# Two kinds of tiles of the first stage mixed three to two, the first two windows loaded between them, and edge loads issued ahead of window loads

## What is computed

```python
h = jnp.concatenate([n_embed[senders], n_embed[receivers]], axis=-1)
h = jnp.tanh(h @ W0 + b0)
h = jnp.tanh(h @ W1 + b1)
h = h @ W2 + b2
h = h * (e_embed @ Wg)
return _segment_mean(h, senders, n_embed.shape[0])
```

## Time and profile before

| | |
|---|---|
| median of 3 runs | 2468.64 us (2465.61 to 2472.03) |
| the profiled execution, own time | 2466.78 us |
| its span, first to last instruction | 2465.0 us |
| first stage, until the last `TB` store has landed | 0 to 97.2 us |
| second stage, first window product to last `first_hidden` | 102.1 to 1603 us |
| mean granted TensorE clock | 0.888 |

### The profile page before, as it was taken

How to read it: one execution, slowest core, us unless ns; L and a number is a source line. 1 busy time by engine, 2 the same in 40 slices (tenths; PEclk the granted TensorE clock), 3 DMA queues, 4 the chain that set the end, 5 groups by cost and what they waited for, 6 DMA issues and landing times.

```text
span 2465.0 us, 41568 instructions
## 1 busy us (share of the span) xinstructions
PE 1989.2 (81%) x12990; PEld 1757.5 (71%) x12990; DVE 1594.8 (65%) x4240; ACT 1416.0 (57%) x2926; POOL 1473.5 (60%) x1204
## 2 busy tenths in 40 slices
PE   7799999999999999999999999945155655555560
PEld 6699889999999999989999989943144444444450
DVE  6466666666666666666666666654266566666575
ACT  2488888888888888888888888834011111111112
POOL 0327777777776777767777777423555555555503
PEclk9899999999999999999999999977567767776785
DMA  6888877777777777777777777574344544444413
GB/s 209 282 208 184 193 165 164 167 163 170 159 158 155 161 158 158 159 157 160 158 160 158 160 159 156 112 186 126 91 113 121 128 112 118 119 119 115 120 48 108
DMA packets 236177, 370.91 MB, mean 150 GB/s; under 512 B 35853, under 2 KB 168935, under 8 KB 235949
## 3 DMA queue, kind: packets, MB, share of 16 engines
q0 software_dynamic: 101232, 188.20, 38.7%
q1 hardware_dynamic: 134717, 179.94, 24.7%
HBM read 270.57 MB, written 97.45 MB: 149 GB/s over the span
## 4 chain that ended last, share of the span: by engine, by line
PE 56%; issue 18%; DVE 11%; ACT 5%; DMA 5%; another core or an unknown queue 4%; POOL 1%; SPq 0%; DVEq 0%; ACTq 0%; POOLq 0%
PE bank L1412 12%; PE bank L1410 12%; PE bank L1411 12%; PE bank L1462 4%; PE bank L1453 4%; DMA accA<-ystage,to_a 3%; PE bank L1479 2%; DVE in_window L860 2%; PE bank L1503 2%; PE bank L1514 2%; PE bank L1504 2%; PE bank L1515 2%; PE bank L1578 1%; ACT drop L1849 1%
## 5 line engine op out<-in xcount | busy, mean ns | idle before, releaser
L1306 POOL DMA_INDIRECT accA<-ystage,to_a x391 | 649.7, 1662 | 233.8 <-issue 111.6
L1312 POOL DMA_INDIRECT GA<-TA,src_c x391 | 426.7, 1091 | 323.3 <-issue 95.4
L1341 POOL DMA_INDIRECT Hg<-HT,src_c x391 | 372.9, 954 | 335.6 <-DVE xb L912 174.8
L1849 ACT ACTIVATE drop<-neg_m 128x1 f32<-128x1 f32 x98 | 28.9, 295 | 613.1 <-issue 348.2
L1410 PE MATMUL bank<-h1h,W1h 128*128 128x512 f32 x882 | 349.2, 396 | 1.5 <-DVE h1l L536 1.4
L1412 PE MATMUL bank<-h1h,W1l 128*128 128x512 f32 x882 | 348.3, 395 | 0.0
L1411 PE MATMUL bank<-h1l,W1h 128*128 128x512 f32 x882 | 347.3, 394 | 0.0
L536 DVE TENSOR_TENSOR h2l<-h2f,h2h 128x512 fp32r<-128x512 f32 (+1 forms) x294 | 202.9, 690 | 202.6 <-issue 78.9
L1607 PE MATMUL bank<-diag,ones 128*128 128x128 f32 x196 | 66.5, 435 | 306.3 <-DVE diag L896 250.2
L1617 PE MATMUL bank<-xb,in_window 128*128 128x260 f32 (+1 forms) x782 | 292.9, 542 | 1.1 <-issue 1.1
L536 DVE TENSOR_TENSOR h1l<-h1f,h1h 128x512 fp32r<-128x512 f32 x294 | 195.1, 691 | 131.3 <-ACT h1h L1686 114.2
(11 more groups left out here) (208 smaller groups left out, 5196.0 us busy)
## 6 DMA issues: line engine op xcount, KB each, us to landing
TW<-TB SPq DMA_DIRECT2D x196, 203.0 KB
ef<-in_eT SPq DMA_DIRECT2D x97, 256.0 KB
bcast_i<-in_src_row SPq DMA_DIRECT2D x97, 256.0 KB
HB<-hist SPq DMA_DIRECT2D x98, 130.0 KB
rel<-RL SPq DMA_DIRECT2D x97, 128.0 KB
rem<-RD SPq DMA_DIRECT2D x48, 256.0 KB
TB<-stB SPq DMA_DIRECT2D x24, 406.0 KB
accA<-zeros SPq DMA_DIRECT2D x4, 1677.0 KB, 13.1
```

What stands on the lines that cost most here:

```text
L1306: return pool.indirect_dma_start(out=table, out_offset=bass.IndirectOffsetOnAxis(ap=rows, axis=0), in_=sums, in_offset=None, compute_op=AL ...
L1312: pool.indirect_dma_start(out=GA[0:n, b % (GAR * BLOCKS_PER_GROUP), :].bitcast(f32), out_offset=None, in_=TA, in_offset=bass.IndirectOffse ...
L1341: pool.indirect_dma_start(out=Hg[0:n, slot, :], out_offset=None, in_=HT, in_offset=bass.IndirectOffsetOnAxis(ap=src_c[0:n, b:b + 1], axis= ...
```

## The change

- `STEPS` is the order of the 50 products: of five steps, the numbers 0, 2 and 4 are senders' tiles and 1 and 3 receivers'. The 25th sender's tile is step 40, steps 41 to 49 are receivers' tiles. TensorE, VectorE and SP follow it; the bank goes by the step.
- ScalarE moves six receivers' tiles ahead of its copies of the weights `W1`, `W2` and `Wg`.
- SP loads window 0 after step 32 (when ten receivers' tiles have landed) and window 1 after step 40. Their first rows are clipped so that they lie in those ten tiles; if a window lay elsewhere, the flag `outside` would send the whole kernel to its slow path. With these edges it stays 0.
- `wait_stage_n0` is split: at the start of the second stage the engines wait for the products alone (`wait_products_n0`), and for the stores (`wait_stores_n0`) at step 1, SP after `ef` and `bcast_i` of group 0. Buffers are laid out anew so that what is written early doesn't lie on `stA` and `stB`.
- In SP's loop window `g + 2` stands behind `ef` and `bcast_i` of group `g`.
- VectorE: one more small operation for `low2_i`, two for `early`, one later for the flag; `h1s` is cleared within the first stage, the constants of `mh` and `ml` at step 1.

```diff
+        early = sb("early", [P, 3])
...
+        EARLY = 10
+        steps_s, steps_r, STEPS = [], [], []
+        while len(STEPS) < 2 * NT:
+            sender = len(steps_s) < NT and len(STEPS) % 5 in (0, 2, 4)
+            (steps_s if sender else steps_r).append(len(STEPS))
+            STEPS.append(("sender" if sender else "receiver", len(steps_s if sender else steps_r) - 1))
+
+        def early_stores(slot):
+            return 16 * sum(len(pieces(t)) for t in range(slot, EARLY, N0R))
...
-        def wait_stage_n0(eng):
+        def wait_products_n0(eng):
+
+            eng.wait_ge(s_n0, 2 * NT)
+            eng.wait_ge(s_n0a, NT)
+            eng.wait_ge(s_n0l, NT)
+            eng.wait_ge(s_rd, 16 * RDS)
+            eng.wait_ge(s_wl, 4)
+
+        def wait_stores_n0(eng):
 
             for k in range(N0R):
                 eng.wait_ge(s_ta[k], stores(N0R, k))
                 eng.wait_ge(s_tb[k], stores(N0R, k))
-            eng.wait_ge(s_rd, 16 * RDS)
-            eng.wait_ge(s_pad, 16)
-            eng.wait_ge(s_wl, 4)
...
-            for t in range(4):
-                sender_bias(t)
+
+            def staged(p):
+                kind, t = STEPS[p]
+                if kind == "sender":
+                    sender_bias(t)
+                else:
+                    receiver_lo(t)
+
+            for p in range(4):
+                staged(p)
...
-            const(dve.tensor_scalar(low2_i[:, :, :], low_all[:, 2:4, :], 2.0, None, ALU.mult), "low_i")
+
+            const(dve.tensor_scalar(low2_i[:, :, TWR:NG], low_all[:, 2:4, TWR:NG], 2.0, None, ALU.mult))
+            const(dve.tensor_scalar(low2_i[:, :, 0:TWR], low_all[:, 2:4, 0:TWR], 2.0, float(2 * EARLY * P - P),
+                                    ALU.mult, ALU.min), "low_i")
...
-            for t in range(4, NT):
-                sender_bias(t)
-                if t == 10:
+
+            const(dve.tensor_tensor(early[:, 0:TWR], low_all[:, 2, 0:TWR], low_all[:, 3, 0:TWR], ALU.max))
+            const(dve.tensor_reduce(early[:, 2:3], early[:, 0:TWR], AX.X, ALU.max))
+            for p in range(4, 2 * NT):
+                staged(p)
+                if p == 20:
...
+                if p == 36:
+                    dve.wait_ge(s_wl, 4)
+                    const(dve.memset(h1s[:, :, :].bitcast(f32), 0.0))
+                if p == 33:
...
-            wait_stage_n0(dve)
-            const(dve.memset(h2l[2 * Q:P, :, 2, :].bitcast(f32), 1.0))
-            const(dve.memset(mh[:, :, :, OUT:OUT + 1].bitcast(f32), 1.0))
-            const(dve.memset(mh[:, :, :, OUT + 1:AW].bitcast(f32), 0.0))
-            const(dve.memset(h1s[:, :, :].bitcast(f32), 0.0))
-            const(dve.memset(ml[:, :, :, OUT:AW].bitcast(f32), 0.0), "ones")
-
-            for s in range(-2, NG + 1):
+            window_hot(0)
+            wait_products_n0(dve)
+            const(dve.memset(h2l[2 * Q:P, :, 2, :].bitcast(f32), 1.0), "ones")
+
+            for s in range(-1, NG + 1):
+                if s == 1:
+                    wait_stores_n0(dve)
+                    const(dve.memset(mh[:, :, :, OUT:OUT + 1].bitcast(f32), 1.0))
+                    const(dve.memset(mh[:, :, :, OUT + 1:AW].bitcast(f32), 0.0))
+                    const(dve.memset(ml[:, :, :, OUT:AW].bitcast(f32), 0.0), "sums' constants")
...
+            const(dve.scalar_tensor_tensor(worst[:, 2:3], early[:, 2:3], float(P - 1 - EARLY * P + HW), worst[:, 2:3],
+                                           ALU.add, ALU.max))
...
-            for t in range(NT):
-                n = rows_of_tile(t)
-                sp.wait_ge(s_n0a, t + 1)
-                for r, e in pieces(t):
-                    sp.dma_start(TA[t * P + r:t * P + e, :], stA[r:e, t % N0R, :]).then_inc(s_ta[t % N0R], 16)
-            for t in range(NT):
-                n = rows_of_tile(t)
-                sp.wait_ge(s_n0l, t + 1)
-                for r, e in pieces(t):
-                    sp.dma_start(TB[t * P + r:t * P + e, :].rearrange("p (k d) -> p k d", k=2),
-                                 stB[r:e, t % N0R, :, :].bitcast(f32)).then_inc(s_tb[t % N0R], 16)
...
-            wait_stage_n0(sp)
-            load_window(0)
-            load_window(1)
+            for p, (kind, t) in enumerate(STEPS):
+                n = rows_of_tile(t)
+                if kind == "sender":
+                    sp.wait_ge(s_n0a, t + 1)
+                    for r, e in pieces(t):
+                        sp.dma_start(TA[t * P + r:t * P + e, :], stA[r:e, t % N0R, :]).then_inc(s_ta[t % N0R], 16)
+                else:
+                    sp.wait_ge(s_n0l, t + 1)
+                    for r, e in pieces(t):
+                        sp.dma_start(TB[t * P + r:t * P + e, :].rearrange("p (k d) -> p k d", k=2),
+                                     stB[r:e, t % N0R, :, :].bitcast(f32)).then_inc(s_tb[t % N0R], 16)
+                if p == 32:
+
+                    for k in range(N0R):
+                        sp.wait_ge(s_tb[k], early_stores(k))
+                    sp.wait_ge(s_xl, PARTS)
+                    sp.wait_ge(s_rd, 16 * RDS)
+                    load_window(0)
+                if p == 40:
+                    load_window(1)
+            wait_products_n0(sp)
             for g in range(NG):
...
-                if g + 2 < NG:
-                    load_window(g + 2)
...
                 sp.dma_start(bcast_i[:, g % 2, 0:n],
                              src_row[g * GE:g * GE + n].partition_broadcast(P)).then_inc(s_bc[g % 2], 16)
+                if g == 0:
+                    for k in range(N0R):
+                        sp.wait_ge(s_tb[k], stores(N0R, k))
+                    sp.wait_ge(s_pad, 16)
+                if g + 2 < NG:
+                    load_window(g + 2)
...
-                t, half = u % NT, u // NT
+                kind, t = STEPS[u]
+                half = 0 if kind == "sender" else 1
                 n = rows_of_tile(t)
                 pe.wait_ge(s_xl, part_of_tile[t] + 1)
                 if u >= 8:
-                    if u - 8 < NT:
-                        pe.wait_ge(s_n0a, u - 8 + 1)
+                    kind, before = STEPS[u - 8]
+                    if kind == "sender":
+                        pe.wait_ge(s_n0a, before + 1)
                     else:
-                        pe.wait_ge(s_n0l, u - 8 - NT + 1)
+                        pe.wait_ge(s_n0l, before + 1)
...
+            def receiver_hi(t):
+                n = rows_of_tile(t)
+                act.wait_ge(s_n0, steps_r[t] + 1)
+                if t >= N0R:
+                    act.wait_ge(s_tb[t % N0R], 16 * (t // N0R))
+                copy(stB[0:n, t % N0R, 0, :], bank_n0(steps_r[t])[0:n, 0:H0]).then_inc(s_n0b, 1)
+
+            for t in range(6):
+                receiver_hi(t)
...
-            for t in range(NT):
-                n = rows_of_tile(t)
-                act.wait_ge(s_n0, NT + t + 1)
-                if t >= N0R:
-                    act.wait_ge(s_tb[t % N0R], 16 * (t // N0R))
-                copy(stB[0:n, t % N0R, 0, :], bank_n0(NT + t)[0:n, 0:H0]).then_inc(s_n0b, 1)
+            for t in range(6, NT):
+                receiver_hi(t)
...
-            wait_stage_n0(act)
-            act.wait_ge(s_dc, DC["ones"])
+            wait_products_n0(act)
...
+                if s == 0:
+                    act.wait_ge(s_dc, DC["ones"])
+                if s == 1:
+                    wait_stores_n0(act)
+                    act.wait_ge(s_dc, DC["sums' constants"])
```

25 lines of the change are left out of this document (11 added, 14 removed).

## The result

The changed kernel takes 2462.5 us (median of 15 runs, 2454.1 to 2470.2), the kernel before beside it 2470.7 us. The ratio is **0.9964, 95% interval 0.9952 to 0.9976**: 0.36% or 9 us less. The forecast was 2443 us, with 2436 to 2454 as its range: 25.6 us less than the kernel before, of which about a third came. One run in all of what follows, of e11, took 2717.8 us against 2441 to 2454 of its other five and is left out of its ratio.

A forecast was written before the change was run, and what follows sets the result against it. TensorE's pace was taken to bound the second stage, whose start waited for the first stage's stores and window load. From 2466.78 us, -19.6 (start) and -6 (edge loads) gave 2441.2, plus 1.9 for the median: 2443 us, range 2436 to 2454.

The forecast's parts named there:

- TensorE's products: First stage: mixed order lets TensorE run without stopping at 1.11 us a product, all done at 76.1 us.
- The gathers come later: First stage's end: last sender's tile moved at 66.8 us, POOL's gathers start at 70.4, the first group lands at 78.3.
- The last nine receivers' tiles: First stage's tail: 1.77 us a tile beside gathers, 25th tile moved at 81.9 us, first window product at about 82.5.
- the rule that the prediction took from the Trainium skill: DMA engines serve queues in turn, a packet each: 2.06 us a tile, start at 83.7 us; not used for the forecast.
- The start as a whole: Second stage's start: first window product at about 82.5 us instead of 102.13, worth -19.6 us.
- rival B: First stage: slower tail or TensorE stalling on full slots, start effectively 5 us later, ef about 1 us; 2453 us, chance 0.18.
- What followed the start: Second stage: runs at TensorE's pace, so an earlier start moves all behind it to the left; no loss was counted.
- Rival C: Second stage: earlier start, but what follows isn't at TensorE's pace; scatters keep the old end; 2462 to 2469 us, chance 0.06.
- two signs of being wrong: Second stage: a first window product behind 90 us, or a period still over 15.5 us, would show the forecast wrong.
- Edge loads a group earlier: Second stage's loop: SP reaches ef a whole group ahead of need, shortening the period; -6 us, bounds 0 and 7.2.
- Rival D: Second stage's loop: the new order makes each group wait on bcast_i; 2491 us at 0.5 us a group, chance 0.03.
- The sum: Whole kernel: 2466.78 - 19.6 - 6 = 2441.2 us profiled; runs' median 1.9 us above, so 2443 us.

The follow-up runs named there:

- e11: Changed kernel with groups 2 to 5 gathered no more than two groups ahead, run in the slower setting; ratio 0.9924 against the kernel before.
- e7: Changed kernel with windows 0 and 1 loaded behind the last TB store, in the faster setting; ratio 0.9932 against the kernel before.
- e10: Changed kernel with windows 0 and 1 behind the last TB store and groups 2 to 5 gathered at most two ahead, slower setting; ratio 0.9938.
- e3: Changed kernel with the gathers of groups 1 to 3 held until VectorE has moved the last receiver's tile, slower setting; ratio 0.9988.
- e9: Changed kernel unchanged, run again in the slower setting; ratio 0.9957 against the kernel before.
- e17: Changed kernel with window 0 after step 40, window 1 after the last store, groups 2 to 5 gathered at most two ahead, slower setting; 0.9927, 2445.8 us.
- e16: Changed kernel with window 0 loaded after step 40 and window 1 after the last TB store, slower setting; ratio 0.9947.
- e18: Changed kernel unchanged, run a third time in the slower setting; ratio 0.9964 against the kernel before.
- e12: Changed kernel with windows 0 and 1 loaded by GpSimd instead of SP, faster setting; ratio 0.9928 against the kernel before.
- e2: Changed kernel with SP's old loop order, window loads ahead of edge loads, from group 1 on, slower setting; ratio 0.9978.
- e14: e6 with window loads ahead of the edge loads again from group 1 on, faster setting; ratio 0.9964 against the kernel before.
- e1: Kernel before with one edit, window g + 2 behind ef and bcast_i of group g in SP's loop, slower setting; ratio 0.9988.
- e4: Changed kernel with the gathers of groups 2 and 3 held until first_hidden(0) is through, slower setting; ratio 0.9975.
- e6: Changed kernel with groups 2 to 5 gathered no more than two groups ahead, run in the faster setting; ratio 0.9935.

## Why the prediction was wrong

**TensorE's products.** Nearly right: done at 78.0 us against 76.1 forecast, with two short stops of 0.4 and 0.6 us. ScalarE's weight copies and the clear cost nothing.

**The gathers come later.** This term was mis-sized. The prediction moved the last sender's tile at 66.8 us; it was moved at 72.4 (70.4 and 70.5 in the other two profiles). It named window 1's hold on SP and forgot window 0's, which stands ahead of step 40 and held SP for 4.1 us, and it left the windows' bytes out of the DMA engines' account from 60 to 78 us. Without them (e7, e10) the move is at 68.1, so the windows are 4.3 of the 5.6 us (2.3 to 2.4 against the other two profiles); the other 1.3 are open. The landing of the group, taken as 3 us between 1 and 6, is 5.3 us here (83.33 to 88.59) and 4.6 to 6.8 us in the experiments: the upper bound was the nearer.

**The last nine receivers' tiles.** From the last sender's move to the last receiver's: 15.1 us forecast, 15.9 measured. The stores took 7 us each and not 3.1, by the chain of waits,

```profile
70.22 6.85 DMA TB<-stB
78.30 7.14 DMA TB<-stB
```

but four slots overlap them. From the tile moved at 77.69 us to the last, five tiles took 10.6 us, 2.1 each, beside gathers; I had 1.77. From 83 to 89 us the queues share nearly alike:

```profile
q1 hardware_dynamic: 403, 1.16, 52.0%
q0 software_dynamic: 318, 1.03, 49.7%
```

By the rule that the prediction took from the Trainium skill (page "DMA: Bandwidth & Descriptors", section "Queues, rings and completion order"), the engines serve the queues in turn, and a tile would take 2.06 us. The trace is near it here: 52.0% to 49.7%, and 2.1 us a tile. The kernel before is not, and not because its gathers had only begun: all sixteen were issued from 60.65 to 80.6 us, and the stores had 57.6% from 66 to 72 us and 60.2% from 72 to 78 us, the gathers 44.8% and 41.2%. What decides between the two shares is not shown, and neither is that the gathers set the tiles' pace: in e3, with four of them beside the tail in place of eight, the last five tiles took 12.5 us (74.03 to 86.54).

**The start as a whole.** First product at 89.4 in place of 82.5, 6.9 us late: 5.6 of it by step 40, 0.8 by the tail, the rest by the hand-overs. Alone this would be rival B ("the tail is slower", or "TensorE's products stall"), whose 5 us were near.

**What followed the start.** This step failed outright: the prediction let the 19.4 us from the first product to `eh(1)` stand, and no term stood for it. They became 28.3 us, since `s_T` came late while sixteen gathers ran out. In the kernel before, the last of the sixteen was issued by 80.6 us, 21 us ahead of the first window product; the change moved them beside the first products of the second stage, for which three engines wait. (The kernel before has a wait that looks alike, ScalarE's 4.19 us until 83.47 among the receivers' tiles, but it can be for a product or for a free slot.) Holding gathers back takes the lateness away (e11 beside e9, e17 beside e16 and e18), so the link to the gathers is shown in the slower setting. Why TensorE's semaphores are held back there, and why not in e12 in the faster one, is not shown. The changed kernel itself didn't run in the faster setting.

Rival C had the time, 2462 to 2469 us, and the words that what is behind the start is not at TensorE's pace, but that is luck: its cause was scatters that keep the old end, and the last scatter came 9.9 us earlier (at 1623.34, before at 1633.24). Neither of the two signs of being wrong came (a first window product behind 90 us, a period over 15.5 us); they looked at the start and at the period, and the loss lay between them.

**Edge loads a group earlier.** Right: 6 us forecast, 6.1 by the traces ((1585.06 - 117.67) / 95 = 15.446 against 15.511), 4.7 to 6.6 by those of e2, e14 and e1; the runs in the slower setting show only 3 to 3.5 us. Rival D was wrong.

**The sum.** -19.6 + 5.6 + 0.8 + 0.5 = -12.7 at the first product; + 8.9 = -3.8 at `eh(1)`; - 6.1 = -9.9 at group 96; the stages behind it took 1.6 us less. Those stages differ by more than 10 us between profiles in the slower setting (from group 96 on 863.9 us in e9, 870.0 before, 874.5 in e3), which is why single profiles and ratios differ by a few us.

## What to carry to other kernels

- When work is moved earlier, redo the account of what runs beside it at its new place. Here a start 13 us earlier came to lie beside sixteen gathers, and 9 us went back.
- A small load put into a full queue is paid for by what is behind it, by the issuer's time (address reads included) and by the time of its packets on the DMA engines. Count every such load ahead of the step that others wait for.
- Prefetch as deep as needed and no deeper at a stage's start; holding it back for good can come due at the stage's end, where the scatters had to drain for 11 us more.

## What the runs showed of the hardware

- In the slower setting, TensorE's semaphore increments reached ScalarE, SP and GpSimd late while twelve to sixteen gathers were under way: ScalarE stood 3.2 to 7.2 us for them. In the changed kernel and in e9 the long wait ended as the DMA engines fell silent (share 0.23 and 0.00 around 101.09, 0.44 around 97.44). That is no rule: the wait until 94.05 ended at a share of 1.01 to 1.10, that of e4 until 108.32 at 0.73. ScalarE's own increments showed no such delay: TensorE started at 94.70, right behind the `tanh` that began at 94.05.
- The two settings differ by some 180 us on one kernel, most of it in the attention stage: its 391 gathers are issued from 1681.8 to 2323.1 us in e9 and from 1676.3 to 2166.8 us in e6, 151 us of the 178 between the two spans. The second stage's period is within 15.45 to 15.46 us in both.
